# A hybrid block of two attentions and two feed-forwards on one core: both halves of the kernel in one software pipeline

## The reference

```
x = x + attn_a(layernorm(x))   # 16 heads of 64: softmax of q over features, of k over tokens;
                               # context = q^T k per head, out = context v, then w_out and b_out
x = x + ffn(layernorm(x))      # xr = mu_r*x + (1-mu_r)*x_prev ; xk likewise with mu_k
                               # sigmoid(xr W_r) * (relu(xk W_k)^2 W_v)
x = x + attn_b(layernorm(x))   # 16 heads of 8, rotary q and k, scores/sqrt(8), softmax, values, W_O
x = x + ffn(layernorm(x))      # the same ffn again
```

## Time and profile before

| | |
|---|---|
| median of 3 runs | 1166.34 us (1165.8 to 1167.78) |
| the profiled execution | 1165.81 us |
| its span in the trace | 1164.0 us |
| mean granted TensorE clock | 0.981 of full speed |
| PE busy | 1019.4 us, 88% of the span |
| ACT busy | 740.4 us, 64% |
| DVE busy | 676.2 us, 58% |
| POOL busy | 427.1 us, 37% |
| DMA | 84.04 MB, mean 72 GB/s |

### The profile page before, as it was taken

The page is one execution under the profiler, slowest core; times in us unless marked ns, Lnnn a source line. Parts: engine busy times, 40 slices in busy tenths (PEclk is TensorE's granted clock), DMA queues, the critical chain, the costliest instruction groups (busy, mean ns, idle before and its releaser), DMA issues.

```text
span 1164.0 us, 23222 instructions
## 1 busy us (share of the span) xinstructions
PE 1019.4 (88%) x8311; PEld 582.1 (50%) x8311; DVE 676.2 (58%) x1620; ACT 740.4 (64%) x857; POOL 427.1 (37%) x338
## 2 busy tenths in 40 slices
PE   4999999999999999649998989998989999999993
PEld 3777777777777777532333333333333333333332
DVE  5788888888888888651334443444344434443334
ACT  3454444444444445318888888887888788878881
POOL 4555555555555555552302231223112311230000
PEclk9999999999999999969999999999999999999997
DMA  5011111111111111222332333233323332232211
GB/s 151 11 56 48 52 42 51 54 54 54 54 54 54 54 54 46 100 93 83 99 101 63 93 100 100 65 88 99 99 65 88 99 99 69 85 101 73 73 37 29
DMA packets 64184, 84.04 MB, mean 72 GB/s; under 512 B 12545, under 2 KB 39042, under 8 KB 64130
## 3 DMA queue, kind: packets, MB, share of 16 engines
q1 hardware_dynamic: 64130, 83.34, 23.8%
HBM read 28.77 MB, written 20.97 MB: 43 GB/s over the span
## 4 chain that ended last, share of the span: by engine, by line
PE 44%; DVE 20%; issue 17%; ACT 11%; POOL 3%; SPq 2%; DMA 2%; DVEq 0%; ACTq 0%; POOLq 0%
PE PS L1227 11%; ACT work L576 9%; PE PS L1208 9%; PE PS L945 5%; DVE work L609 4%; PE PS L950 3%; DVE q_sum L648 3%; PE PS L1056 3%; PE PS L952 3%; PE PS L951 3%; DVE st L591 2%; PE PS L1017 2%; DVE qk_norm L722 2%; PE PS L1065 1%; DMA qkv_back<-qkv_scratch 1%
## 5 line engine op out<-in xcount | busy, mean ns | idle before, releaser
L576 ACT ACTIVATE work<-PS 128x1024 f32<-128x1024 f32 x512 | 489.2, 1026 | 103.7 <-PE PS L1208 102.2
L1227 PE MATMUL PS<-work,v 128*32 128x512 f32 x2048 | 273.6, 606 | 1.1 <-ACT work L576 1.1
L1208 PE MATMUL PS<-q_st,k_st 32*128 32x512 f32 x1024 | 203.3, 498 | 40.6 <-ACT work L576 32.8
L1208 PEld LDWEIGHTS PS<-q_st,k_st 32*128 32x128 f32 x1024 | 80.1, 182 | 207.7 <-ACT work L576 167.9
L342 POOL TENSOR_TENSOR work<-work,q_rcp 128x1024 f32<-128x1024 f32 x64 | 122.3, 1912 | 89.8 <-DVE q_rcp L652 89.8
L331 POOL TENSOR_TENSOR rs<-ve,half_neg 128x4 f32<-128x4 f32 x64 | 66.1, 1033 | 240.2 <-DVE ve L602 240.2
L466 ACT ACTIVATE work<-PS 128x1024 f32<-128x1024 f32 x64 | 65.6, 1026 | 137.5 <-PE PS L952 137.5
L404 POOL TENSOR_TENSOR v<-qkv_back,one 128x512 f32<-128x512 f32 x16 | 16.6, 1040 | 265.7 <-PE PS L1227 265.7
L950 PE MATMUL PS<-work_r,h1h 128*128 128x512 f32 x256 | 109.1, 426 | 5.2 <-POOL h1l L337 3.4
L952 PE MATMUL PS<-work_r,h1l 128*128 128x512 f32 x256 | 102.0, 399 | 0.0
L951 PE MATMUL PS<-work_r,h1h 128*128 128x512 f32 x256 | 101.7, 397 | 0.0
(11 more groups left out here) (145 smaller groups left out, 1557.8 us busy)
## 6 DMA issues: line engine op xcount, KB each, us to landing
qkv_scratch<-qkv_sb SPq DMA_DIRECT2D x16, 768.0 KB, 3.2
qkv_back<-qkv_scratch SPq DMA_DIRECT2D x16, 768.0 KB, 4.6
work<-in_attn_a_x SPq DMA_DIRECT2D x32, 256.0 KB, 3.1
x_scratch<-x SPq DMA_DIRECT2D x16, 256.0 KB, 2.1
k_st<-k_hi SPq DMA_DIRECT2D x64, 64.0 KB, 2.1
k_st<-k_lo SPq DMA_DIRECT2D x64, 64.0 KB, 2.1
q_st<-q_hi SPq DMA_DIRECT2D x64, 64.0 KB, 2.1
q_st<-q_lo SPq DMA_DIRECT2D x64, 64.0 KB, 2.1
```

Of the source, the lines that this page charges most:

```text
L576: act.activation(probs[s % NC][:, 2 * t:2 * t + 2, :], PS[:, 2 * t:2 * t + 2, :], ACT.Exp).then_inc(s_exp.sem, 1)
L1208: mm = pe.matmul(PS[:, h, :], k_st[g % 2][rows, kc * P:(kc + 1) * P], q_st[g % 2][rows, :], start=True, stop=not guarded, tile_position=(3 ...
L1227: mm = pe.matmul(PS[32 * h:32 * h + 32, 4 + u, :], v_flat[p][:, kc, at:at + 32], probs[kc][:, h, :], start=(n % 8 == 0), stop=(n % 8 == 7) ...
```

## The change

The two halves become one pipeline of 20 steps. `iterations` writes out 5 steps, a loop of four turns of two steps (5 to 12), and 7 more. Step `i` holds, each where that batch exists: A = attention A of batch i; S = output of A and ffn 1 of batch i-1; L = projections, rotary turn and split for attention B of batch i-2; B = the scores of batch i-3; E = output of B and ffn 2 of batch i-4. So all five are there in steps 4 to 15, 12 of the 20. Every step is 16 slots `n`, and in each slot PE does one `proj_half` (one 512-column part of q or k), the scores of slot n, what `fused` lists for that slot, and the values of slot n-1.

- `scores` issues its four tiles at once, into banks 0 to 3, behind one wait for one exponential of 2048 columns. In the steps without A (16 to 18) they are split in pairs again.
- `proj_half` has one bank (4) while B runs, which transposes, `ffn_k` and a few more share with it, each behind waits for the one before.
- The expanded exponentials and probabilities have 2 buffers instead of 4, U has one, the split halves of q and k one set.
- The second half reads q, k and v from SBUF, no longer from the DRAM scratch; they are still stored there. `x2` is loaded back as before.
- The ffn: ACT copies the transposed h to SBUF, POOL takes the difference of neighbouring tokens, DVE forms both mixes from SBUF, DVE does the relu, POOL the square. The rotary sum moves from POOL to DVE, the copy of `h1T` from ACT to DVE.
- The guarded versions of A and of B are written without a pipeline. That of B stands behind the 20 steps and runs over them only where `bounded_b` says no; the norms are still gathered, and judged in step 18.

```diff
-def over_batches(eng, step, n, tail, last=1):
...
+        def iterations(eng, step):
+            for i in range(5):
+                step(i, i % 2)
+            with eng.Fori(5, 13, 2) as i:
+                step(i, 1)
+                step(i + 1, 0)
+            for i in range(13, FUSED):
+                step(i, i % 2)
...
+            def exp_half(a, n, alone):
+                c, r = n // 4, n % 4
+                if r == 0:
+                    hold(act, c_mm, a, c - 1)
+                hold(act, ph_mm, a, n + 1)
+                bank = n % 4 if alone else 4
+                act.activation((EQ, EK)[r // 2][c % 2][:, (r % 2) * 512:(r % 2) * 512 + 512], PS[:, bank, :], ACT.Exp)\
+                   .then_inc(ph_exp.sem, 1)
+            def exp_scores(z, b, n):
+                hold(act, z["pv"], b, n - 1)
+                hold(act, z["s_mm"], b, n + 1)
+                act.activation(probs[n % 2], PS[:, 0:4, :], ACT.Exp).then_inc(z["s_exp"].sem, 1)
...
+            def mix(f, j):
+                hold(dve, f["d"], j)
+                for n in (1, 0):
+                    dve.scalar_tensor_tensor(mixed[n][:, :], diff[:, :], mu[:, n:n + 1], hT_sb[:, 0:N], ALU.mult, ALU.add)\
+                       .then_inc(f["mix"].sem, 1)
...
+            def scores(z, b, n):
+                hold(pe, z["s_exp"], b, n)
+                for h in range(4):
+                    rows = slice(32 * h, 32 * h + 32)
+                    mm = pe.matmul(PS[:, h, :], k_st[g % 2][rows, kc * P:(kc + 1) * P], q_st[g % 2][rows, :],
+                                   start=True, stop=True, tile_position=(32 * h, 0))
+                mm.then_inc(z["s_mm"].sem, 1)
...
+            def fused(i, p):
+                for n in range(16):
+                    if A:
...
+                        if E and n == 3:
+                            hold(pe, z["ct_sb"], e)
...
+                        if E and n == 11:
+                            hold(pe, f2["relu"], e)
+                        if B and n == 12:
+                            hold(pe, z["u_norm"], b, 2)
+                        if E and n == 13:
+                            hold(pe, f2["x"], e, 1)
+                        if B and n == 14:
+                            hold(pe, f1["relu"], s)
+                        proj_half(a, p, n, not B)
+                    if B and A:
+                        scores(z, b, n)
+                    if B and not A:
+                        scores_split(z, b, n)
...
+                    if n == 14 and S:
+                        if L:
+                            hold(pe, z["split"], l)
+                        ffn_r(f1, s)
...
+                    if B and n >= 1:
+                        weigh_values(z, b, n - 1, 1 - p)
```

More of the change, by code:

```diff
@@ new lines, in guarded_a, with guarded_b @@
+            def guarded_a(j):
+                for c in range(NC):
+                    exp_q(j, c)
+                    exp_k(j, c)
+                t_copy(j)
+                m_copy(j)
+                h_copy(ffn[0], j)
+                gates(ffn[0], j)
+                hold(act, qkv_st, j - 1)
+                for c in range(NC):
+                    p_copy(j, c)
+            def guarded_b(i):
+                for n in range(16):
+                    exp_scores(att[1], i, n)
+                h_copy(ffn[2], i)
+                gates(ffn[2], i)
@@ new lines, in guarded_a @@
+            def guarded_a(j, p):
+                k_maxima(j)
+                k_shift(j)
+                for c in range(NC):
+                    q_shift(j, c)
+                    hold(dve, q_exp, j, c + 1)
+                    q_sums(j, c)
+                c_norm(j)
+                add_x1(j)
+                ln_norm(1, j, x1, hn)
+                mix(ffn[0], j)
+                relu(ffn[0], j, 4)
+                end_ffn1(j)
+                ln_norm(2, j, x2, h3)
+                split_h3(j)
@@ new lines, in guarded_b @@
+            def guarded_b(i):
+                z, f = att[1], ffn[2]
+                rope_sum(z, i)
+                split_kq(z, i, 0)
+                split_kq(z, i, 1)
+                for u in range(2):
+                    maxima(i, 2 * u)
+                    maxima(i, 2 * u + 1)
+                    pv_copy(z, i, u)
+                    normalise(z, i, u, 7)
+                cT_copy(z, i)
+                add_x3(z, 4, i)
+                ln_norm(4, i, x3, hn)
+                mix(f, i)
+                relu(f, i, 4)
+                gate_v(f, i, 4)
+                hold(dve, z["out_st"], i - 1)
+                add_gated(f, i, x3, out_sb)
@@ new lines, in guarded_a @@
+            def guarded_a(j, p):
+                f = ffn[0]
+                head_kmax(j, p)
+                for c in range(NC):
+                    proj_q(j, p, c)
+                    proj_k(j, p, c)
+                    if c == 0:
+                        hold(pe, kx_ok, j)
+                    hold(pe, k_exp, j, c + 1)
+                    context(j, c)
+                hold(pe, p_ev, j - 1)
+                ctx_wout(j)
+                wv_ctx_wout(j)
+                attn_out(j, p)
+                ffn_T(f, 1, j)
+                hold(pe, f["hc"], j)
+                ffn_k(f, j)
+                ffn_r(f, j)
+                hold(pe, f["gate"], j)
+                ffn_v(f, j, 7)
+                hold(pe, f["x"], j, 1)
+                h3_transposes(j)
+                for c in range(NC):
+                    proj_b(j, c)
@@ new lines, in guarded_b @@
+            def guarded_b(i):
+                z, f = att[1], ffn[2]
+                hold(pe, f["gate"], i - 1)
+                kq_T(z, i, 0)
+                hold(pe, z["split"], i, 2)
+                kq_T(z, i, 1)
+                hold(pe, z["split"], i)
+                for n in range(16):
+                    if n % 4 == 0:
+                        maxima(z, i, n // 4)
+                    scores_shifted(z, i, n)
+                    weigh_values(z, i, n, 0)
+                    if n % 8 == 7:
+                        u_transposes(z, i, n // 8, 7)
+                        hold(pe, z["u_norm"], i, 2 * (n // 8) + 2)
+                hold(pe, f["x"], i - 1, 1)
+                c_transposes(z, i)
+                heads_out(z, i)
+                ffn_T(f, 4, i)
+                hold(pe, f["hc"], i)
+                ffn_k(f, i)
+                ffn_r(f, i)
+                hold(pe, f["relu"], i)
+                ffn_v(f, i, 4)
```

1561 lines of the change are left out of this document (806 added, 755 removed).

## The result

The changed kernel takes 1186.88 us (median of 4 runs, 1185.9 to 1187.31). The kernel before takes 1167.06 us beside it (4 runs, 1165.8 to 1168.17). The ratio is 1.0169, with a 95% interval of 1.0151 to 1.0187. The change makes the kernel 1.7% slower. The forecast was 1065 us, faster at 0.95, so both the time and the sign were wrong, and 1186.88 lies outside the range of 1012 to 1125.

The account below looks back on a forecast made before the run. PE was taken to bound each step: 57.6 us of work plus waits, between 60.7 and 64.6, taken as 63; twelve such steps (756) and the first and last ones gave 1062.5, forecast 1065 us, own range 1035 to 1100.

Parts of the forecast that it names:

- the forecast 5.4: Waiting of PE in a full step: 63 us taken for the step, over 57.6 us of PE work.
- wait in slot 13: PE waits for the end of ffn 2: 0.8 us, or 3.2 if POOL's squares of the norms go first.
- the one in slot 11: PE waits for the relu of ffn 2: 0.3 us, or 1.8 if POOL's next operation keeps DVE out first.
- the 0.9 of slots 2 and 3: PE waits behind DVE's list from the end of ffn 1: 0.6 us, and 0.3 for h3 in slot 3.
- the splits: Slots 13 and 14: transposes of q wait for the split of k, `ffn_r` for that of q; 1.1 us together.
- PE in a full step: PE's work in a step with all five parts, summed from start-to-start times of the earlier trace: 57.6 us.
- The part of q or k: One 512-column part on PE: 0.75 us, half of two parts at 1.50; 16 are 12.0 us a step.
- The check by the first half: The same PE sum for a first-half batch, 27.3 plus 2.4 idle, gives 29.7 us, close to the 29.0 to 29.6 taken.
- The sum: All steps added, first to last, with steps 4 to 15 at 63 us each: 1062.5 us, 1065 as forecast.
- step 2: Early step with A, S and L but no scores: 31 us, like a first-half step with the longer ffn chain.
- Rival 3: DVE and POOL never run side by side, DVE is the bound at 74 us a step; total 1197, slower. Chance 0.03.
- Rival 2: DVE and POOL block each other more than counted, half landing on PE; step 66 to 71, total near 1125. Chance 0.19.

Follow-up runs that it names:

- e11: e9 with GpSimd's difference of ffn 1 moved before the split of h1 and the copy of v; 1069.73 us, ratio 0.9146 to the kernel before.
- e3: The changed kernel with the value matmul of ffn 2 made three times instead of once in slot 12; 1161.8 us, ratio 0.9956 to the kernel before.
- e2: The changed kernel with its twenty steps written out, no hardware loop; 1173.11 us, ratio 1.0059 to the kernel before.
- e1: The changed kernel with GpSimd waiting for the mixes after each of its two differences; 1136.65 us, ratio 0.9753 to the kernel before.
- e4: The changed kernel with both GpSimd waits of e1 and the written-out steps of e2; 1115.2 us, ratio 0.9568 to the kernel before.
- e7: The changed kernel with only the second wait of e1, before GpSimd's squares; 1144.76 us, ratio 0.9808 to the kernel before.
- e5: e4 with DVE's relu of ffn 2 before attention A's q sums and the rotary sum; 1148.87 us, ratio 0.9842 to the kernel before.
- e9: e5 with DVE's split of k and gating of ffn 2 before the mixes of ffn 1; 1089.53 us, ratio 0.932 to the kernel before.
- e10: e4 with the split of k and gating before the mixes of ffn 1, without the early relu; 1114.13 us, ratio 0.9534 to the kernel before.
- e12: e11 without the two waits that hold GpSimd behind the mixes; 1100.51 us, ratio 0.9428 to the kernel before.
- e6: e4 with the scores of every step made and exponentiated in two pairs of tiles; 1118.2 us, ratio 0.9573 to the kernel before.

## Why the prediction was wrong, step by step

**What held.** The period did lie above what PE, ACT, DVE or POOL need alone. The exponential took 1.88, four score tiles 0.43, and PE waited for no stack in the middle. The two large waits stood where they had been followed, at slots 11 and 13, and the sum was close: 5.1 us a step for the forecast 5.4. That sum was partly luck. The wait in slot 13 came out at its blocked end (3.0 for 0.8 or 3.2), the one in slot 11 between its ends (1.1 for 0.3 or 1.8), one that was not forecast came in slot 10 (0.8 for `mixed_r`), and against them the 0.9 of slots 2 and 3 did not come at all and the splits took 0.2 for 1.1. The mixes took 1.33 to 2.19 us on the mean beside GpSimd's operations, so the mixes of both ffn were blocked, where the prediction took a value between the two ends. The Trainium skill, "SBUF — State Buffer", section "SBUF: two separate sides", says that a DVE operation with two SBUF inputs and a GpSimd operation that reads SBUF lock each other out for a whole instruction. By these 1.33 to 2.19 us the trace agrees.

**"PE in a full step": 57.6 was 60.5.** The step that holds the size of the content. e11 measures it. The part of q or k, 0.75 by the earlier trace rows, costs 0.89 where it stands alone between the values and the scores. The 0.75 was the mean of two parts in a row, and in the trace of before the second of the two starts here:

```profile
246.08 0.39 PE L950 MATMUL PS<-work_r,h1h 128*128 128x512 f32 x1
```

So the first part took 246.08 - 245.28 = 0.80, and the second, behind a part like itself, 246.78 - 246.08 = 0.70. In the new order no part has another one before it: its first matmul holds PE for 0.34, and its last, before the score tiles, for 0.33:

```profile
434.88 0.50 PE L1054 MATMUL PS<-wqk,h1h 128*128 128x512 f32 x1
435.22 0.40 PE L1055 MATMUL PS<-wqk,h1h 128*128 128x512 f32 x1
435.46 0.40 PE L1056 MATMUL PS<-wqk,h1l 128*128 128x512 f32 x1
435.79 0.50 PE L1191 MATMUL PS<-q_st,k_st 32*128 32x512 f32 x4
```

From 434.88 to 435.79 are 0.91. At 16 parts this is 2.3 us, and the chunk of B's projection (0.71 for 0.56) adds 0.6. The check by the first half (27.3 + 2.4 = 29.7 for 29.0 to 29.6) could not see it, because there the parts do stand in pairs. Both sizes hold as measured; why a matmul takes longer behind another kind was not tested.

**The clock was counted at nothing.** It was listed in no term. The earlier trace rows had 1.00 in both halves and 0.77 between them, which showed that the clock falls where PE idles, and the prediction read the 42 us between the halves only as idle time that goes. In the changed kernel each step has a stop of 2.9 us, and behind nearly all of these a stretch at 1.2 GHz: 64.9 us between A's outputs in steps 4 and 16. e3 prices it at about 1.5 us a step.

**The loop jump was counted at nothing.** Loops were there before, with their jumps at another spot. In the new loop a turn has 12.6 / 3 = 4.2 us of PE waiting for issue, with the lower clock after it, and the step is 7 us longer (74 for 67). e2 prices all turns at 14 us, and the pair e1 and e4 at 21.

Together for a middle step without a jump: 60.5 + 5.1 of waits, and 1.6 that is left for the clock, make 67.2 for the measured 67.3. The 1.6 is a remainder, close to the 1.5 of e3. The three jumps and the shorter last interval bring the mean to 68.5.

**"The sum": the first and last steps were 50 us too short.** The prediction put the point from which the kernel is slower at 71.4 us a step, with 307 us for the rest. Outside the stretch between A's outputs in steps 4 and 16 the kernel took 1185.5 - 821.9 = 364 us, where the forecast has 313.5, and by the same formula the point lies at (1164 - 364) / 12 = 66.7. The mean of 68.5 is then slower. It took both misses to turn the sign: with the middle as it was and the ends as forecast the span is 821.9 + 313.5 = 1135, with the ends as they were and the middle as forecast 364 + 749 = 1113, both under 1164. The forecast of step 2 (31 us, "a step of the first half with the longer ffn chain") failed most: A's output comes 40.0 and 53.9 us after the one before, where the sum gives 29 and 40. All chains run there and no scores cover them:

```profile
98.91 4.67 DVE L683 TENSOR_SCALAR hn<-x,mom,rs 128x128 f32<-128x128 f32 x4
...
112.19 2.36 DVE L748 SCALAR_TENSOR_TENSOR mixed_k<-diff,mu,hT_sb 128x512 f32<-128x512 f32 x1 [6.12 <-POOL diff L386]
...
116.60 0.69 PE L1050 MATMUL PS<-ident,qk_rot 128*128 128x128 f32 x2 [8.01 <-DVE k_lo L790]
```

The layernorm of four operations stands behind three GpSimd operations in a row and takes 4.67 for its free 1.12; the split of k stands behind mixes that wait for the difference, and PE stops for 8.0. In e11, whose order takes such places apart, the two steps take 36.0 and 46.8. The last 157 us have their waits too (8.8 for `mixed_r`, 5.1 for `hn`, 3.9 for `k_lo`), for the forecast's 136.5. There too the blocked mixes are about half of the miss: with both waits on GpSimd (e1) this stretch takes 145.9 us, with the second alone (e7) 153.9, and the waits for `mixed_r` are 3.9 and 8.7 us. The `hn` wait of 5.1 stays in both. The cause of the other 9 us stays open; e11 still has 147 there.

**The rivals.** Rival 3 had the right sign by the wrong way: DVE is busy 370 of 600 us in the middle, far from being the bound, and GpSimd 247, and for 151 of the 600 both have an instruction in flight, blocked time counted. Rival 2 had a mechanism that is shown, and its step of 66 to 71 was what came, but the blocking alone does not make that step (without it e1 has 64.2, and 71 at a jump), and on 307 us of rest it gave 1125. The error was to attach the chance of "slower" to one mechanism, while three smaller terms that all point one way (content, clock, jump) and the ends were held at their best value.

## What to carry to other kernels

When two pipelines are put into one, every in-order list becomes longer, and what counts is what stands ready behind a waiting instruction. Follow each list for operations whose input is there while their engine idles, and put those first; the three reorderings of e5, e9 and e11 together won 45 us on e4 with no work removed. Size pieces from rows in which they stand between the same neighbours as in the new order, and size the first and last steps with their own chains, not by scaling the full one.

Price a stop of TensorE with the clock behind it. Behind stops of 1 us (e9, e11) it did not fall in the middle, behind 2.0 us it fell in half of the steps or more (e4, e10), behind 2.9 and 4.2 us in nearly all. An edit that trades a short stop for a longer one loses, as e5 did, and a change of order can be judged only with its partner.

## What the runs showed of the hardware that was not expected

- Holding an idle engine back made the kernel faster. Two waits on GpSimd gave 50 us (e1), 42 of them by one of the two (e7), and 31 in the good order (e12). A wait can also only move the block: with the sine products held, the mixes were free and the layernorm behind them took 639 ns an operation for 337.
- Useless matmuls in a stop paid for themselves: 1.8 us of work in a step, and a step without a jump 1.5 us shorter (e3).
- A `scalar_tensor_tensor` of two SBUF operands takes 0.75 us free and up to 2.37 beside GpSimd, and ends about 0.55 us after GpSimd's operation; successive GpSimd operations can each stop one burst (4.67 for 1.12).
- The jump of the hardware loop over a body of two steps stops TensorE twice, by up to 2.0 and 2.7 us, and makes the step 7 us longer than its neighbours. Writing the steps out took away 14 us (e2), or 21 (e1 to e4), of three jumps.
- Score tiles on separate 32-row groups issued as two pairs back to back hold TensorE for 0.43 us, like four under one semaphore (e6).
